# Rewriting the order of work in the last layer of a two-layer kernel on one Trainium2 core

## The reference, cut to what matters

```python
xn = _layernorm(x)                                   # 4 x 512 x 128
x = x + _L1_attn_ref(xn, ...) + _L1_ffn_ref(xn, ...)

# _L1_attn_ref: a state-space scan, 256 hidden channels, 16 states each
u = x @ W_x.T + b_x
g = sigmoid(x @ W_g.T + b_g)
h = conv3(u) + conv_b                                # 3 taps along the tokens, per channel
u = u * g + h * (1 - g)
dt = clip(softplus(x @ W_dt.T + b_dt).mean(axis=(0, 1)), 0.001, 2.0)   # one step width per channel
A = -softplus(A_raw);  A_d = exp(A * dt);  B_d = (A_d - 1) / (A + 1e-6) * B_ssm
# state[t] = A_d * state[t-1] + B_d * u[t];  y[t] = sum_s C_ssm * state[t]
out = layernorm(x + y @ W_out.T + b_out) * ln_g + ln_b

# _L1_ffn_ref: 8 experts, each token takes two
gates = softmax(xt @ gate_w);  two best: sel, tok_w = sum of the two
y_e = gelu(xt @ w1[e] + b1[e]) @ w2[e] + b2[e]
out = sum_e sel[e] * tok_w * y_e
```

## Time and profile before

| what | value |
|---|---|
| median of 3 runs | 442.86 us (442.4 to 443.07) |
| profiled execution, its own time | 440.8 us |
| its span, first to last instruction | 439.0 us |
| busy share of the span | PE 87%, DVE 70%, ACT 65%, POOL 42% |
| mean granted clock of PE | 0.961 |
| `layer1` in the span | from 298.69 us to the end |
| first scan instruction of `layer1` | 386.62 us |

### The profile page before, as it was taken

The page is one execution under the profiler, slowest core; times in us unless marked ns, Lnnn a source line. Parts: engine busy times, 40 slices in busy tenths (PEclk is TensorE's granted clock), DMA queues, the critical chain, the costliest instruction groups (busy, mean ns, idle before and its releaser), DMA issues. The chain is left out here.

```text
span 439.0 us, 10304 instructions
## 1 busy us (share of the span) xinstructions
PE 383.9 (87%) x3196; PEld 269.8 (61%) x3196; DVE 305.5 (70%) x1065; ACT 287.0 (65%) x690; POOL 182.6 (42%) x301
## 2 busy tenths in 40 slices
PE   1999998988999999999987899969788669698993
PEld 0544343457888888888875577756243345576983
DVE  4657709554888888888874578866969985474185
ACT  4687668554666766666653767656589952995634
POOL 1404909105898898988968323232000030000013
PEclk9999999998999999999999999999699789898998
DMA  8230332261222222222245300000000010000003
GB/s 234 41 86 16 93 90 91 78 181 51 55 64 74 72 60 65 66 72 72 54 120 160 66 1 2 1 0 0 1 1 1 0 23 4 1 1 0 1 1 96
DMA packets 33004, 23.01 MB, mean 52 GB/s; under 512 B 10046, under 2 KB 32716, under 8 KB 32972
## 3 DMA queue, kind: packets, MB, share of 16 engines
q1 hardware_dynamic: 31724, 22.54, 19.1%
q10 hardware_dynamic: 1248, 0.07, 0.2%
HBM read 13.13 MB, written 9.47 MB: 51 GB/s over the span
## 5 line engine op out<-in xcount | busy, mean ns | idle before, releaser
L479 PE MATMUL bank<-w,hT 128*128 128x385 f32 x128 | 45.4, 495 | 0.4 <-ACT stage L606 0.4
L976 ACT ACTIVATE win<-bank 128x384 f32<-128x384 f32 (+1 forms) x124 | 42.9, 396 | 0.0
L895 PE MATMUL bank<-win,wst 128*32 128x128 f32 x1024 | 41.0, 279 | 1.3 <-ACT kd L969 1.3
L479 PEld LDWEIGHTS bank<-w,hT 128*128 128x128 f32 x128 | 23.2, 189 | 24.5 <-issue 11.4
L895 PEld LDWEIGHTS bank<-win,wst 128*32 128x32 f32 x1024 | 31.6, 110 | 5.6 <-ACT kd L969 1.5
L1472 POOL TENSOR_TENSOR win<-win,lng 128x512 f32<-128x512 f32 x2 | 2.5, 1268 | 71.2 <-ACT win L1757 71.2
L1244 ACT ACTIVATE std_<-mv_,cst 128x2 f32<-128x2 f32 (+1 forms) x46 | 13.5, 296 | 25.4 <-DVE mv_ L1222 14.2
L985 ACT ACTIVATE bstd<-bmv,cst 128x1 f32<-128x1 f32 x32 | 9.4, 295 | 30.8 <-DVE bmv L1087 30.8
L1036 POOL TENSOR_SCALAR xh<-raw,bmv,brs 128x128 f32<-128x128 f32 x32 | 25.4, 793 | 2.9 <-DVE brs L1091 2.8
L1952 POOL MEMSET region<- 128x4096 f32 x1 | 3.5, 3512 | 51.9 <-ACT region L1714 51.9
L1490 PE MATMUL bank<-xn1T,w1e 128*128 128x512 f32 x32 | 17.7, 673 | 7.2 <-ACT he L1651 5.7
(11 more groups left out here) (307 smaller groups left out, 1175.7 us busy)
## 6 DMA issues: line engine op xcount, KB each, us to landing
rows_scratch<-stage SPq DMA_DIRECT2D x32, 192.5 KB
win<-rows_scratch SPq DMA_DIRECT2D x32, 192.5 KB, 2.4
attn_scratch<-ob SPq DMA_DIRECT2D x32, 64.0 KB
att<-attn_scratch SPq DMA_DIRECT2D x4, 512.0 KB, 4.2
xt<-in_L_attn_x SPq DMA_DIRECT2D x4, 256.0 KB, 4.2
out<-win SPq DMA_DIRECT2D x4, 256.0 KB, 2.4
cst<-in_constants SPq DMA_DIRECT2D x1, 408.0 KB, 5.1
w<-in_L_attn_wk SPq DMA_DIRECT2D x2, 128.0 KB, 4.3
```

The lines of the kernel that those rows point to most:

```text
L479: mm = nc.tensor.matmul(rows_bank(i, h)[:, 0:RC], hT[:, k, i * P:(i + 1) * P], w4[:, k, h, :], start=(k == 0), stop=(k == 1))
L895: mm = nc.tensor.matmul(dst[32 * b:32 * b + 32, 0:F], v[:, at:at + 2 * K], w_sb[:, state, first_slot(b) + h, :], start=False, stop=(h == 1 ...
L976: nc.scalar.activation(w_sb[:, state, at:at + n, :], bank[b][:, 0:n * F].rearrange("f (h g) -> f h g", h=n), ACT.Copy).then_inc(w_done, 1)
```

## The change

What it does, part by part:

- `layer0_out`: the copy into `xn1T` also sums each feature over the tile's tokens (`accum_out`, 16 times), and POOL rescales the convolution's weights and the gate's bias once (`halve`).
- The softplus of the step width is |x|/2 + x/2 + ln(1 + exp(-|x|)). The eight max(x, 0) instructions go: |x| is summed by its own instruction, and the sum of x comes from the tile sums through two small products of W_dt.
- The order: PE and ACT begin with the step width (`magnitude`, `decayed`), then take the logarithms, and only then the gates and gelus. The decays (`decay`) are made on DVE ahead of the first `blend`.
- The gate: with the weights halved, `cv` holds (h - u)/2, and u g + h (1 - g) = (tanh(-z/2) + 1) (h - u)/2 + u. `gate_tile` is one ACT instruction with Tanh; `blend` is one `scalar_tensor_tensor` on DVE, and POOL adds u and writes `uT`. ACT makes no tap any more: `conv` is three instructions on DVE.
- `ub`, `cv` and `gate` have four slots (RING = 4), u has one PSUM bank, the picks come one at a time in two banks.
- ACT's list takes gelu n, gate n and, for n < 4, `u_tile(4 + n)` in turn. The functions are ordered exp, ln, gelu with tanh, exp, gelu, sqrt.
- POOL spreads the decay over `d0` and makes the tap blocks `wtap` (before: ACT). The memset of `region2` covers 4096 elements at the start (before: 2048 of `gt` at the start and 4096 in the middle).
- The exponentials of the decay (t1, a32, kex, ex2 and the eight of win) stand in one place on ACT, between expert tiles 7 and 8; before, two of them stood between tiles 3 and 4 and the others behind tile 11.

The diff, cut to its core:

```diff
 layer0_out
+                            ins = nc.scalar.activation(xn1T[:, i * P:(i + 1) * P], bank[6 + p][:, 0:P], ACT.Copy,
+                                                       accum_out=m1.xsum[:, i:i + 1])
 layer1, PE
+                dt_product(0)
+                for i in range(NT):
+                    nc.tensor.matmul(bank[7][:, i * NE:(i + 1) * NE], xn1T[:, i * P:(i + 1) * P], m1.gate_w[:], start=True, stop=True)
+                for k in range(2):
+                    mm = nc.tensor.matmul(bank[7][:, NT * (NE + k):NT * (NE + k + 1)], wT[:, 2, half(k)], m1.xsum[:], start=True, stop=True)
+                mm.then_inc(gate_mm, 1)
+                dt_product(1)
+                u_product(0)
+                for n in range(2, NU):
+                    dt_product(n)
+                    if n in (3, 5, 7):
+                        u_product(n // 2)
+                gate_product(0)
+                gate_product(1)
+                up(0, 0)
+                up(0, 1)
+                pe.wait_ge(gates_done, 1)
+                turn_gates(0)
+                turn_gates(1)
+                u_product(4)
+                for i in (2, 3):
+                    pe.wait_ge(gT_done, i - 1)
+                    turn_gates(i)
                 for n in range(NU):
+                    if n + 2 < NU:
+                        up(*divmod(n + 2, 4))
+                        gate_product(n + 2)
+                    if n < 3:
+                        u_product(5 + n)
+                    pick(n)
                     if n == 5:
+                        down(0)
+                for q in range(4):
+                    up(2, q)
+                    pick(8 + q)
+                    if q == 1:
+                        down(1)
                 down(2)
 layer1, ACT
 def u_tile(n):
+                    if n >= RING:
+                        act.wait_ge(uT_done, n - RING + 1)
+                    nc.scalar.activation(ub[:, n % RING, 1:L + 1], bank[0][:, :], ACT.Identity, ...).then_inc(u_done, 1)
+                for n in range(NU):
+                    hidden(*divmod(n, 4))
+                    gate_tile(n)
+                    if n < 4:
+                        u_tile(4 + n)
+                nc.scalar.activation(t1[:], lna[:], ACT.Exp) ... a32, kex, ex2, then the eight of win
                 for q in range(4):
-                    tap_blocks(q)
+                    hidden(2, q)
 layer1, DVE
+                gate_logits()
                 conv(0)
                 gates()
+                for n in range(1, RING):
+                    conv(n)
+                    if n == 1:
+                        gate_rows(0)
+                        gate_rows(1)
+                gate_rows(2)
+                gate_rows(3)
+                decay()
+                for n in range(NU):
                     blend(n)
+                    if n < RING:
+                        conv(n + RING)
+                    apply_gate(n)
+                    if n == 5:
+                        turn_inputs(0)
+                    if n == 6:
+                        add_experts(0)
                 ... five small instructions from t1 to cbc ...
+                turn_inputs(1)
+                add_experts(1)
                 ... two products of kex, a reduce ...
+                apply_gate(8)
                 ... two transposes into x2 ...
+                apply_gate(9)
+                nc.vector.tensor_tensor(ex2[:], ex2[:], cbc[:, :, None].broadcast_to([P, NG, TC]), ALU.mult)
+                apply_gate(10)
+                apply_gate(11)
                 add_experts(2)
 layer1, POOL
+                nc.gpsimd.memset(region2[:], 0.0).then_inc(pool_stage, 1)
+                for n in range(NU):
+                    pool.wait_ge(blend_done, n + 1)
+                    nc.gpsimd.tensor_tensor(uT[:, k, row(b)], cv[:, p, :], ub[:, p, 1:L + 1], ALU.add).then_inc(uT_done, 1)
+                pool.wait_ge(gT_done, 4)
+                nc.gpsimd.memset(gt[:, :, :, 0:2], 0.0).then_inc(pool_stage, 1)
+                pool.wait_ge(a32_done, 1)
+                nc.gpsimd.tensor_copy(d0[:, :, :, 1:NCH], a32[:, :, None, None].broadcast_to([P, NG, B, NCH - 1])).then_inc(d0_done, 1)
+                pool.wait_ge(x2_done, 2)
+                for q in range(4):
+                    nc.gpsimd.tensor_copy(wtap[quad(q), :, quad(q)], x2[quad(q), :, :].rearrange("p c j -> p j c")).then_inc(taps, 1)
```

More of the change, by code:

```diff
@@ L1622, in _ @@
                 up(3, 1)
-                picks(3, (0, 1))
+                pick(12)
+                pick(13)
                 for m in range(4, 8):
@@ L1627, in _ @@
                 up(3, 3)
-                picks(3, (2, 3))
+                pick(14)
+                pick(15)
                 pe.wait_ge(wst_done, 8)
@@ L1679, in _ @@
+                magnitude(2)
+                magnitude(3)
                 u_tile(1)
[L1680 to L1689 removed]
@@ L1690, in _ @@
-                u_tile(3)
-                for n in range(NU):
-                    b, k = divmod(n, 2)
-                    act.wait_ge(dt_mm, n + 1)
-                    nc.scalar.activation(ab[:, n, :], bank[4 + n % 2][:, :], ACT.Abs, bias=m1.bd[:, k:k + 1]).then_inc(abs_done, 1)
-                    if n:
-                        act.wait_ge(relu_done, n)
-                    nc.scalar.activation(rl, bank[4 + n % 2][:, :], ACT.Relu, bias=m1.bd[:, k:k + 1],
-                                         accum_out=dtr[:, k, b:b + 1]).then_inc(relu_done, 1)
-                    if n in (2, 5):
-                        u_tile(4 + n // 5)
@@ L1702, in _ @@
[L1702 to L1709 removed]
+                decayed(0)
+                magnitude(4)
+                magnitude(5)
+                u_tile(2)
+                magnitude(6)
+                magnitude(7)
+                decayed(1)
@@ L1723, in _ @@
+                nc.scalar.activation(ex2[:], ex2[:], ACT.Exp).then_inc(ex2_stage, 1)
                 act.wait_ge(lna_in, 128)
@@ new lines, in conv @@
+                    dve.wait_ge(u_done, n + 1)
+                    nc.vector.tensor_scalar(cv[:, p, :], ub[:, p, 0:L], cw[:, k, 0:1], cb[:, k:k + 1],
+                                            ALU.mult, ALU.add).then_inc(conv_done, 1)
+                    for tap in (1, 2):
+                        dve.wait_ge(conv_done, 3 * n + tap)
+                        nc.vector.scalar_tensor_tensor(out=cv[:, p, :], in0=ub[:, p, tap:L + tap], scalar=cw[:, k, tap:tap + 1],
+                                                       in1=cv[:, p, :], op0=ALU.mult, op1=ALU.add).then_inc(conv_done, 1)
@@ L1833, in _ @@
                 w(nc.vector.tensor_scalar(bsp[:], a_raw[:], 0.0, None, ALU.max))
+                gate_logits()
                 conv(0)
-                blend(0)
-                conv(1)
-                blend(1)
                 gates()
-                for n in range(2, NU):
+                for n in range(1, RING):
                     conv(n)
-                    blend(n)
-                    if n in (2, 3):
-                        gate_rows(2 * n - 4)
-                        gate_rows(2 * n - 3)
-                    if n >= 6:
-                        apply_gate(2 * n - 12)
-                        apply_gate(2 * n - 11)
```

291 lines of the change are left out of this document (114 added, 177 removed).

## The result

The changed kernel takes 456.47 us, median of four runs (456.09 to 457.19), the kernel before 442.97 (442.4 to 444.31): ratio 1.0302, interval 1.0275 to 1.0329. The forecast was 445.6 in a range from 440.0 to 451.0. The direction was right, the size was not: +13.5 us, where the sum said +2.7.

What follows compares the result with a forecast made beforehand. The prediction took the bound to be a chain of waits through ACT and DVE as much as PE. Its terms, 1.0 + 1.3 (scan start) + 0.4 = +2.7 on 442.86, gave 445.6 us, range 440.0 to 451.0.

Steps and rivals of the forecast that it cites:

- `layer0_out`, +1.0: In `layer0_out`, sum reads behind the 16 copies add at most 1.4 us to the loop's path; 1.0 taken.
- To the first blend: From `layer1`'s start through step width, convs, choice of experts and decay: first `blend` starts at b 31.0.
- Tiles 0 to 3: Expert tiles 0 to 3 in `layer1`: four steps of 5.46 us each, so blend 4 starts at b 53.6.
- The ring: Tiles 0 to 3: blend, POOL's addition, `u_tile(4 + n)`, conv and `apply_gate` wait on each other, 5.46 us a step.
- The 0.75 that I gave the clock: Before tiles 0 to 3: PE's idle lowers its clock, making u 5 and pick 0 late by 0.75 us.
- Tiles 4 to 7: Blend 4 at b 53.6, a transposition until 60.5, blend 7 and its gate until 64.1, t1's chain until 69.3.
- Tiles 8 to 11: Second transposition until b 72.9, `apply_gate(9)` 77.4, ex2's product waits 1.55 us for a `wtap` copy, `apply_gate(11)` ends 81.0.
- The wait for down 2: Behind `apply_gate(11)`: DVE waits 6.45 us, as before, for the down product's end, until b 87.4.
- The tail, +0.4: Behind the scan's start: picks 14 and 15 wait for `apply_gate(12)` and (13), making `chunk_out` 0.4 us later.
- That GpSimd does not hold DVE: First rival: POOL's work does not hold DVE, 4.5 us of holds go, 441.1 us; chance 0.20.
- That all four copies hold ex2's product: Third rival: POOL's four `wtap` copies run without letting DVE in, 6.0 us more, 451.6 us; chance 0.18.
- That the clock stays up: Second rival: no clock loss behind gate logits, in tiles 0 to 3 or in down 2, 442.0 us; chance 0.13.

Runs made afterwards that it cites:

- the clock kept: Changed kernel plus 14 TensorE products whose results nobody reads, placed where TensorE stood idle: 450.73 us, ratio 1.02 to the kernel before.
- the ring opened: Changed kernel with six places for u and eight for the convolution in place of four: 445.14 us, 1.0019 of the kernel before.
- pairs and clock: Changed kernel, four slots kept, with picks issued two by two and 14 unread TensorE products: 450.09 us, 1.0135 of the kernel before.
- the ring opened with copies on ScalarE: Changed kernel with six u and eight convolution places, `d0` and `wtap` copies moved from GpSimd to ScalarE: 443.84 us, 0.9941 of before.
- the tail's order alone: Changed kernel with only TensorE's tail reordered, `up(3, 2)`, `up(3, 3)` and picks 14, 15 behind first `chunk_out` products: 450.5 us, 1.013 of before.

## Why the prediction was wrong in size, step by step

**`layer0_out`, +1.0:** right; 0.8 by the turns. The rest of the 4.75 is mainly the lower clock from about 240 to 253 us, which the kernel before has too in other executions (4.37 later there, without the change). Taking the median as base was right for that reason, which I did not know: that was luck. Nor can a measurement of this kernel tell 0.9 us from three runs, as I had put it: ten runs lie 5.8 apart.

**To the first blend:** b 30.99 for 31.0, with its waits where they were put. (In other executions, among them the clock kept, the ring opened, and pairs and clock, it came at b 32.7, where TensorE stayed longer at its lower level behind the gate logits. That is not the edits' doing: the ring opened with copies on ScalarE had 31.0, the tail's order alone 32.7.)

**Tiles 0 to 3: this is the step that failed.** The ring was right, and at the upper clock so was its price: 22.4 for four steps with the clock kept, against 4 x 5.46 = 21.8, and three waits of 0.18 for a pick are the difference. Wrong was "PE's products (3.0 of 5.46) are covered; if PE stays at the lower level through all four steps it costs 1.5 more", in price and in path. The price: a step has u, pick, `up` and gate product; 3.0 less three products of 0.86 leaves 0.4 for the pick, under half of what it takes alone. The 1.13 in the earlier trace rows that I called four picks is two (x4). With the ring opened the four products take 3.8 from start to start; at the lower level, 337.13 to 344.79 above, they take 7.7, more than the ring. The path: pick n stands behind a u product that waits for the ring's `u_tile`, so the ring runs through TensorE too. At the lower level that way is the longer one, 7.49 in the first step. The 0.75 that I gave the clock became 0.75 + 2.7.

**Tiles 4 to 7:** the same step again, +4.7 to the start of cbc. I priced it on DVE's list alone, with a wait of 0.4 for pick 6; `apply_gate(4)`, (5) and (6) waited 3.47, 1.68 and 0.81. TensorE has no u product here, but `up`, gate product and pick take 5.7 from pick 3 to pick 4 at the lower level, 3.0 with the clock kept. With the clock kept, 2.1 of the 4.7 stay, with pairs as well 0.8.

**Tiles 8 to 11:** GpSimd's holds had the right size: `d0` 3.41 on the product (3.5), `wtap` 2.04 on ex2's (2.0 a copy, 1.55 of it waited; 1.35 measured), addition 7 about 0.8. New was 1.79 for pick 11, behind pick 10 and `up(11)` at 2.0 each. The wait for down 2 is 6.45, the very number carried over from before; that it fits is luck, since other runs here had 4.8 to 7.5.

**The tail, +0.4:** +1.2. Behind the first scan, picks 14 and 15 began 0.7 later than before (13.4 against 12.7), and from their start to `chunk_out` it was 1.62 in place of 1.06. The sum's 0.5 for a pick stands in no row. That `chunk_out` could start ahead of the last scan I did not see.

Together: 2.7 + 4.7 + 1.8 in the block and 0.8 behind it, 10.0; the medians ask for 10.8. The ends of the prediction's own sum, half taken, give 444.0 to 448.1 and not 443.5 to 449; the measured time lies outside either.

**Rivals.** That GpSimd does not hold DVE is refuted by three rows. That all four copies hold ex2's product is refuted by 2.04. That the clock stays up did not happen; I priced it at 3.6 (445.6 to 442.0), and keeping it was worth 5.7. What was priced too low was its opposite, the clock staying down: the sum's ends held 1.5 for it, not worked out on TensorE's own list.

The Trainium skill (SBUF — State Buffer, Who interferes with whom) has the second instruction wait for the whole of the first; the product of t1, 376.01 to 379.42 beside a copy that ended at 379.38, agrees. Its rule on strided reads (GPSIMD Engine Reference, Performance pitfalls for Q7 kernels) had given my estimate of 2.5 us; 8.23 for four is 2.06, and the measurement decides.

## What to carry to other kernels

Price an instruction in the company that it will have: four picks of two rows side by side took 1.14, one alone 1.12. Follow a new wait through every engine that has work behind it: here DVE's ring had a second way through TensorE. When a change adds a wait that idles TensorE, add up all that TensorE does in one step at the lower clock and compare it with the step; if it is longer, TensorE is the next bound. And undo the wait first: opening the ring took off 11.3, the two mends behind it together 6.4.

## Not expected of the hardware

- Picks in different row groups run side by side in pairs and fours: 1.12 for one, 1.13 for two, 1.14 for four; at the lower level 2.07 for one and 2.08 for two.
- The granted clock falls in `layer0_out` in some executions of the same kernel and not in others: mean 0.941 to 0.972 and 439.07 to 444.88 us over ten runs of the kernel before.
- A one-input `tensor_scalar` of 32 elements took 1.01 beside GpSimd's addition, 0.17 with the additions on VectorE; the two later taps of a conv took 2.25 to 2.43 beside one (ring opened) and 1.54 without.
